# Four-unit attention groups with contexts stored as columns: products of V joined, a wider mask on TensorE, reads of K and Q moved forward

## The chip, the cores and the metric

One core of a Trainium2 chip runs the kernel. The metric is the device time of one execution in microseconds (us). The profiler's names for the engines are PE (TensorE, with PEld for its weight loads), DVE (VectorE), ACT (ScalarE), POOL (GpSimd) and SP (SyncE, which here issues the DMAs).

## The reference

Input x has shape (2, 2048, 512), all in float32. Four blocks follow one another:

```python
# embed: a domain adapter
h = gelu(x @ down.T + b); h = h @ expert[domain].T + ...; x = layernorm(h @ up.T + b + x)
# attention, 16 heads of 32 columns, 2048 queries and keys, 2 batches
y = ln(x) * (1 + scale) + shift
q, k, v = heads(y @ Wq + bq), heads(y @ Wk + bk), heads(y @ Wv + bv)
scores = q @ k.T / sqrt(32) + attention_bias          # bias (2, 16, 2048, 2048)
probs = softmax(where(mask, -inf, scores))
y = y + (probs @ v) @ Wo + bo
# feed-forward 512 -> 2048 -> 512, then a rotation of column pairs and a gated low-rank correction
y = y + gelu2(ln(y) @ W1 + b1) @ W2 + b2
```

The bias alone is 512 MB and is read once.

## The kernel before

The program has three stages, each a block with one instruction list per engine and semaphores between them: `embed_stage`, `attention_stage`, `ffn_stage`. No scheduler is at work. The order on each engine is the order of the calls in the loops at the end of each engine's function.

**Attention** works in units. A unit is 128 queries of one head against all 2048 keys, and there are 512 of them: 2 batches, 2 halves of the queries, 16 heads, 8 units (`RING`). Per unit:

- SP reads the 1 MB tile of the bias into one of eight `tiles` (L1186, L1099) when PE has transposed what was in it.
- POOL adds the negative mask to the first 1920 columns (`pool_columns`, L1249).
- PE computes the scores in two halves (`qk`, L1267), each of two matmuls of 512 columns, into the one score tile `ps_s` in PSUM. To the last 128 columns PE also adds the mask with a matmul of the identity (L1273).
- DVE adds scores and bias and takes the row minimum, one half at a time (`scores`, L1409). PE's next scores of the same half wait for it.
- ACT computes the exponential of the row with its sum (`exp`, L1349).
- PE transposes the probabilities in four chunks of four 128x128 blocks into three PSUM banks in turn (`transposes`, L1288). ACT or DVE copies each chunk to SBUF (`take`, L1359 and L1420). A bank is free for the next chunk but two when it is copied.
- For each pair of units PE multiplies with V (`pv`, L1307). Keys are split in halves, so that two halves of two units fill the four column groups of 32: 32 matmuls, 64 rows in the trace.
- DVE copies the four parts (`parts`, L1444), PE transposes them (`parts_rows`, L1315), and DVE takes reciprocals of the two sums and forms the contexts as rows (`context`, L1428, L1430, L1437). ACT stores them when the sixteen heads are done.

Around a head's eight units SP reads K and Q of the next head (`load_kq`, eight DMAs, L1104 and L1105) behind the first bias tile, and V behind the third.

**FFN** works in eight tiles of 512 tokens. `ctx_columns` (L1787) transposes a tile of contexts, 16 transposes into `ps_t`; ACT copies them (`take_ctx`, L2156); `out_project` (L1975) multiplies with Wo. Then follow the weight products, with weights read in cards of 256 KB, twelve ahead (L1719).

Of the kernel before, what the change touches and what calls it, by code (L numbers as in the profile page):

```python
# [30 lines left out]
P = 128  # L31
# [1016 lines left out]
def attention_buffers(nc, net, ctx, place):  # L1048
# [13 lines left out]
    at.pool_columns = S - 128  # L1062
# [9 lines left out]
    at.p_t = [sb(f"at_prob_t{i}", [P, 2, S // P, P]) for i in range(2)]  # L1072
# [5 lines left out]
    at.cx_sb = sb("at_ctx_parts", [P, P])  # L1078
    at.cx_all = sb("at_ctx_rows", [P, RING, D])
    at.rmin = sb("at_rmin", [P, RING, 2])  # L1080
    at.rsum = sb("at_rsum", [P, RING])
    at.rinv = sb("at_rinv", [P, 2])
# [35 lines left out]
def attention_stage(nc, net):  # L1118
# [9 lines left out]
    NP = NU // 2  # L1128
    KT = S // P
    CH = S // 512  # L1130
    QUART = KT // 2
    TB = 3

# [7 lines left out]
    with ExitStack() as ctx:  # L1141
# [7 lines left out]
        cx_sb, cx_all, rmin, rsum, rinv = net.at.cx_sb, net.at.cx_all, net.at.rmin, net.at.rsum, net.at.rinv  # L1149
# [13 lines left out]
        s_cxs = sem("at_ctx_parts_ready")  # L1163
        s_cxm = sem("at_ctx_summed")
        s_cxo = sem("at_ctx_ready")
        s_rv = sem("at_rinv_ready")
        s_st = [sem(f"at_ctx_stored{i}") for i in range(RING // 2)]
# [9 lines left out]
        def _(sp):  # L1177
# [17 lines left out]
            def load_v(n):  # L1195
                _, _, b, qh, h = place(n * RING)
                after(sp, s_pv, 4 * (n - 1))
                at.read_v(sp, n % 2, b, h)
# [8 lines left out]
            def load_ffn():  # L1207

                for i in range(2):
                    sp.wait_ge(s_st[i], 16)  # L1210
                    sp.wait_ge(s_st[i + 2], 16)
                sp.dma_start(net.cx[:], net.ctx.rearrange("(t j p) d -> t p j d", j=TJ, p=P)[0]).then_inc(net.s_cx, 16)
# [10 lines left out]

            for u in range(at.early, RING):
# [15 lines left out]
            load_ffn()  # L1240

# [11 lines left out]
        def _(pe):  # L1253
# [37 lines left out]
            def pv(pr):  # L1291
                if not 0 <= pr < NP:
                    return

                n = pr * 2 // RING
                after(pe, s_cxo, 2 * pr)
                if pr % 4 == 0:
                    pe.wait_ge(s_vin[n % 2], 16 * (n // 2 + 1))
                for u in (2 * pr, 2 * pr + 1):
# [3 lines left out]
                for i in range(QUART):  # L1303
                    for g in range(4):
                        half, j = divmod(g, 2)
                        t = half * QUART + i
                        last = pe.matmul(ps_c[g * HD:(g + 1) * HD, 0:P], v_sb[n % 2][:, t, :], p_t[pr % 2][:, j, t, :],  # L1307
                                         start=(i == 0), stop=(i == QUART - 1))
                last.then_inc(s_pv, 1)

            def parts_rows(pr):
                if not 0 <= pr < NP:
                    return
                pe.wait_ge(s_cxs, pr + 1)
                pe.transpose(ps_c[:, P:2 * P], cx_sb[:], ident).then_inc(s_cxm, 1)  # L1315

            for g in range(-1, NU // 4 + 1):
                u, pr = 4 * g, 2 * g
                transposes(u, (0, 1))
                qk(u + 3, 1)  # L1320
                parts_rows(pr - 2)
                transposes(u, (2, 3))
                qk(u + 4, 0)
                transposes(u + 1, (0, 1, 2))
                pv(pr - 1)
                qk(u + 4, 1)
                qk(u + 5, 0)
                transposes(u + 1, (3,))
                transposes(u + 2, (0, 1))
                qk(u + 5, 1)  # L1330
                parts_rows(pr - 1)
                transposes(u + 2, (2, 3))
                qk(u + 6, 0)
                transposes(u + 3, (0, 1, 2))
                pv(pr)
                qk(u + 6, 1)
                qk(u + 7, 0)
                transposes(u + 3, (3,))

        @block.scalar  # L1340
        def _(act):
            cxv = net.ctx.rearrange("(b q t p) c -> (b q) p t c", p=P, t=RING, q=QH)

# [8 lines left out]
            def take(u, c):  # L1352
# [3 lines left out]
                pr, j = divmod(u, 2)  # L1356
                after(act, s_pv, pr - 1)
                act.wait_ge(s_pt[k], i + 1)
                act.activation(p_t[pr % 2][:, j, 4 * c:4 * c + 4, :].rearrange("p t q -> p (t q)"), ps_p[k][:],  # L1359
                               ACT.Copy).then_inc(s_pe[k], 1)  # L1360

            def store(pr):
                if not 0 <= pr < NP:
                    return
                if (pr // 4) % HEADS == HEADS - 1:
                    act.wait_ge(s_cxo, 2 * pr + 2)
                    of = slice(2 * (pr % 4), 2 * (pr % 4) + 2)
                    act.dma_start(cxv[pr // (4 * HEADS)][:, of, :], cx_all[:, of, :]).then_inc(s_st[pr % 4], 16)

            for g in range(0, NU // 4 + 1):  # L1370
                u, pr = 4 * g, 2 * g
                take(u - 2, 2)
                take(u - 2, 3)
                exp(u)
                take(u - 1, 1)
                exp(u + 1)
                take(u - 1, 3)
                take(u, 0)
                take(u, 1)
                take(u, 2)  # L1380
# [1255 lines left out]
```

## Time and profile before

| what | value |
|---|---|
| median of 3 runs (lowest, highest) | 3473.58 us (3472.29, 3478.68) |
| the profiled execution, and its span | 3475.8 us, 3474.0 us |
| mean granted clock of TensorE | 0.992 |
| busy: PE, PEld | 3408.8 us (98%), 2692.7 us (78%) |
| busy: DVE, ACT, POOL | 2343.6 us (67%), 2278.9 us (66%), 2395.8 us (69%) |
| embed, attention, FFN, by the first matmul of each stage | to 490.3, to 2495.6, to the end |
| read from HBM, written | 849.63 MB, 99.62 MB |

Attention is 58% of the span, FFN 28%. An engine's busy time is what its instructions took; PE's rows overlap, so the distance from one start to the next tells more than a duration. A line "A <- B" in a list of waits gives how long A stood idle until B released it.

### The profile page before, as it was taken

The numbers are of one execution on the slowest core, as the hardware profiler recorded it, in microseconds if no ns is written. First come the engines' busy times: TensorE is split into PE (matmuls) and PEld (weight loads), VectorE is DVE, ScalarE is ACT, GpSimd is POOL, SyncE is SP. The second block draws the span as 40 slices with busy tenths as digits, with TensorE's granted clock in tenths as the row PEclk, the third lists the DMA queues.
The fourth block names the chain that finished last, engine by engine and source line by source line (L and its number), as shares of the span: only waits on it lengthen the run. The fifth ranks groups of instructions, "written<-read, shape, count | busy, mean of one in ns | idle before, by whom it ended". The sixth has DMA issues, their size and how long they took to land. (4 is left out here: it accounts for less than half of the span.)

```text
span 3474.0 us, 84659 instructions
## 1 busy us (share of the span) xinstructions
PE 3408.8 (98%) x33299; PEld 2692.7 (78%) x33299; DVE 2343.6 (67%) x5039; ACT 2278.9 (66%) x3399; POOL 2395.8 (69%) x942
## 2 busy tenths in 40 slices
PE   7999989999999999999999999999999999999998
PEld 3444448888888888888888888888778888887886
DVE  7776758888888888888888888888623232332333
ACT  2433449999999999999999999999622212221321
POOL 1222249999999999999999999999643324232322
PEclk8999999999999999999999999999999999999998
DMA  6666599888898988898888998888644544564463
GB/s 215 225 235 239 197 367 349 325 337 331 333 401 329 338 331 333 341 389 337 332 332 329 367 370 334 331 327 329 246 144 154 167 137 157 164 191 143 154 210 124
DMA packets 342721, 954.80 MB, mean 275 GB/s; under 512 B 33204, under 2 KB 190004, under 8 KB 267576
## 3 DMA queue, kind: packets, MB, share of 16 engines
q1 hardware_dynamic: 337108, 940.95, 73.4%
q10 hardware_dynamic: 5220, 8.42, 0.6%
q8 instruction: 269, 4.41, 0.5%
q14 instruction: 124, 1.02, 0.1%
HBM read 849.63 MB, written 99.62 MB: 273 GB/s over the span
## 5 line engine op out<-in xcount | busy, mean ns | idle before, releaser
L1249 POOL TENSOR_TENSOR at_tiles<-at_tiles,at_negmask 128x1920 f32<-128x1920 f32 x509 | 1950.7, 3896 | 29.9 <-DMA at_tiles<-in_bias 19.0
L1349 ACT ACTIVATE at_tiles<-at_tiles,at_rmin 128x2048 f32<-128x2048 f32 x512 | 1030.5, 2013 | 2.4 <-DVE at_rmin L1409 2.4
L1288 PE MATMUL at_ps_p<-consts,at_tiles 128*128 128x128 f32 x8192 | 1023.6, 272 | 1.7 <-ACT at_prob_t L1359 1.3
L1288 PEld LDWEIGHTS at_ps_p<-consts,at_tiles 128*128 128x128 f32 x8192 | 936.3, 139 | 72.5 <-DVE at_prob_t L1420 2.0
L1359 ACT ACTIVATE at_prob_t<-at_ps_p 128x512 f32<-128x512 f32 x1664 | 898.2, 603 | 125.0 <-PE at_ps_p L1288 124.9
L1409 DVE CUSTOM_DVE_ANT_0 at_tiles<-at_ps_s,at_tiles,at_rmin 128x1024 f32<-128x1024 f32 x512 | 655.0, 1279 | 171.7 <-PE at_ps_s L1273 171.0
L1267 PE MATMUL at_ps_s<-at_k_stack,at_q_stack 128*128 128x512 f32 x2048 | 700.7, 438 | 8.1 <-DVE at_rmin L1409 6.1
L1409 DVE CUSTOM_DVE_ANT_0 at_tiles<-at_ps_s,at_tiles 128x1024 f32<-128x1024 f32 x512 | 623.9, 1219 | 24.5 <-POOL at_tiles L1249 22.2
L1307 PE MATMUL at_ps_c<-at_prob_t,at_v 128*32 128x128 f32 x16384 | 500.3, 274 | 1.0 <-DVE at_ctx_rows L1437 1.0
L1307 PEld LDWEIGHTS at_ps_c<-at_prob_t,at_v 128*32 128x32 f32 x16384 | 431.6, 110 | 44.2 <-issue 43.0
L1267 PEld LDWEIGHTS at_ps_s<-at_k_stack,at_q_stack 128*128 128x128 f32 x2048 | 310.8, 191 | 62.5 <-issue 51.5
L1420 DVE COPY at_prob_t<-at_ps_p 128x512 f32<-128x512 f32 x384 | 251.9, 683 | 3.0 <-PE at_ps_p L1288 3.0
L1863 PE MATMUL ff_ps_m<-ff_norm_t,ff_w_card 128*128 128x256 f32 x1024 | 234.7, 379 | 1.4 <-ACT ff_feats L2147 0.9
L1863 PEld LDWEIGHTS ff_ps_m<-ff_norm_t,ff_w_card 128*128 128x128 f32 x1024 | 194.2, 190 | 31.1 <-issue 3.3
L2276 POOL TENSOR_TENSOR ff_x<-ff_res,ff_b 128x512 f32<-128x512 f32 x32 | 46.4, 1473 | 229.0 <-DVE ff_x L2447 229.0
L2160 ACT ACTIVATE ff_norm_t<-ff_ps_t,ff_beta_columns,ff_g_columns 128x512 f32<-128x512 f32 (+1 forms) x36 | 23.3, 728 | 255.5 <-PE ff_ps_t L1787 240.2
L633 ACT ACTIVATE em_qk<-em_ps_q,em_bqk 128x512 f32<-128x512 f32 x64 | 44.0, 687 | 190.5 <-PE em_ps_q L446 172.0
L1273 PEld LDWEIGHTS at_ps_s<-at_negmask,ident_bf 128*128 128x128 bf16 x512 | 48.9, 96 | 137.8 <-issue 137.8
L693 POOL TENSOR_TENSOR em_gs_norms<-em_gs_norms,em_half 128x2 f32<-128x2 f32 x32 | 27.9, 871 | 167.1 <-DVE em_gs_norms L747 167.1
L2252 POOL TENSOR_TENSOR ff_hid_sum<-ff_hid_c,ff_hid_d 128x512 f32<-128x512 f32 x32 | 40.6, 1268 | 146.2 <-ACT ff_hid_c L2110 146.2
L2095 ACT ACTIVATE ff_part_m<-ff_ps_m 128x512 f32<-128x512 f32 x32 | 19.1, 597 | 172.9 <-PE ff_ps_m L1863 172.9
L2390 DVE TENSOR_TENSOR ff_hid_c<-ff_ps_m,ff_part_u 128x512 f32<-128x512 f32 x32 | 22.1, 691 | 162.9 <-PE ff_ps_m L1863 162.9
(239 smaller groups left out, 4098.3 us busy)
## 6 DMA issues: line engine op xcount, KB each, us to landing
at_tiles<-in_bias SPq DMA_DIRECT2D x512, 1024.0 KB, 6.3
ff_w_card<-w_mix SPq DMA_DIRECT2D x256, 256.0 KB, 2.7
ff_w_card<-in_W SPq DMA_DIRECT2D x192, 256.0 KB, 2.9
at_k_stack<-k_hi SPq DMA_DIRECT2D x128, 256.0 KB, 5.6
at_k_stack<-k_lo SPq DMA_DIRECT2D x128, 256.0 KB, 5.6
negm<-em_mask_out SPq DMA_DIRECT2D x32, 512.0 KB, 6.5
at_q_stack<-q_hi SPq DMA_DIRECT2D x128, 128.0 KB, 5.3
at_q_stack<-q_lo SPq DMA_DIRECT2D x128, 128.0 KB, 5.3
```

The source lines that it names most:

```text
L633: act.activation(qk32[:, i % 2, :], ps_q[g % 3][:], ACT.Identity, bias=bqk[:, k, c:c + 1]).then_inc(s_qk32, 1)
L1249: pool.tensor_tensor(tiles[s][:, 0:PCOLS], tiles[s][:, 0:PCOLS], negm[s][:, 0:PCOLS], ALU.add).then_inc(s_pool, 1)
L1267: last = pe.matmul(out, q_st[n % 2][:, s * P:(s + 1) * P], k_st[n % 2][:, c * 512:(c + 1) * 512], start=True, stop=not masked)
L1273: last = pe.matmul(ps_s[:, lo:(c + 1) * 512], net.ident_bf[:], negm[s][:, lo:(c + 1) * 512], start=False, stop=True)
L1288: last = pe.transpose(ps_p[k][:, y * P:(y + 1) * P], tiles[s][:, t * P:(t + 1) * P], ident)
L1307: last = pe.matmul(ps_c[g * HD:(g + 1) * HD, 0:P], v_sb[n % 2][:, t, :], p_t[pr % 2][:, j, t, :], start=(i == 0), stop=(i == QUART - 1))
L1349: act.activation(tiles[s][:, :], tiles[s][:, :], ACT.Exp, bias=rmin[:, s, 1:2], scale=-1.0, accum_out=rsum[:, s:s + 1]).then_inc(s_exp, 1)
L1359: act.activation(p_t[pr % 2][:, j, 4 * c:4 * c + 4, :].rearrange("p t q -> p (t q)"), ps_p[k][:], ACT.Copy).then_inc(s_pe[k], 1)
L1409: v.tensor_tensor_reduce(out=half, in0=ps_s[:, a * HALF:(a + 1) * HALF], in1=half, scale=-1.0, scalar=-MAX_FLOOR if a == 0 else rmin[:, s, ...
L1420: v.tensor_copy(p_t[pr % 2][:, j, 4 * c:4 * c + 4, :].rearrange("p t q -> p (t q)"), ps_p[k][:]).then_inc(s_pe[k], 1)
L1863: last = pe.matmul(bank[:, h * HALF:(h + 1) * HALF], left[:, k, h * P:(h + 1) * P], right[:, k, :], start=(m in (1, 2, 5) and h == 0 and k ...
L2276: pool.tensor_tensor(x2[:, j, :], res[:, j, :], b2, ALU.add).then_inc(s_x2, 1)
```

## The change

- Contexts are formed for four units at once. Each of the 16 key blocks of V is multiplied with the probabilities of four units, one per column group, 64 matmuls in one run (128 rows in the trace). The result is the contexts as columns: head dimension and unit on the partitions, queries along the row. No sum of parts is left.
- The probabilities now stand in five single buffers, not two double ones.
- The four row sums get their reciprocals on DVE (`invert`), a copy spreads each over 32 columns, PE transposes the tile (`rinv_columns`), DVE copies it from PSUM (`take_rinv`), and one DVE product of 128 columns gives the contexts (`context`). SP stores them, 64 KB a group, in blocks by head.
- POOL's part of the mask ends at column 1856; PE adds it for 192 columns.
- K and Q of the head after next are read behind the sixth bias tile of each head, and those of the second head ahead of the loop.
- PE's, ACT's and DVE's calls stand in another order; the scores lead the transposes by four units.
- FFN reads a context tile with 16 DMAs in the form that `out_project` needs. The transposes, ACT's copies and their semaphores go. The two banks that `out_project` writes first are swapped in some tiles (`row_bank`).

```diff
-    at.pool_columns = S - 128
+    at.pool_columns = S - 192
-    at.p_t = [sb(f"at_prob_t{i}", [P, 2, S // P, P]) for i in range(2)]
+    at.p_t = [sb(f"at_prob_t{i}", [P, S // P, P]) for i in range(4)]
+    at.p_t += [sb("at_prob_t4", [P, S // P, P])]
+            load_kq(1)
             for n in range(NH):
...
-                        if s == 0:
-                            load_kq(n + 1)
+                        if s == 5 and n + 2 < NH:
+                            load_kq(n + 2)
                         if s == 2:
                             load_v(n + 1)
+                        if s % 4 == 2:
+                            store(2 * n + s // 4 - 1)
...
+            def store(g):
+                n, s, b, qh, h = place(4 * g)
+                sp.wait_ge(s_cxo, g + 1)
+                sp.dma_start(net.ctx[(b * QH + qh) * 2 + s // 4, h], cx_t[g % 2][:]).then_inc(s_st[g % 2], 16)
...
+            def pv(g):
+                pe.wait_ge(s_rc, g + 1)
...
+                for t in range(KT):
+                    for j in range(4):
+                        last = pe.matmul(ps_c[j * HD:(j + 1) * HD, 0:P], v_sb[n % 2][:, t, :], p_t[(4 * g + j) % NPT][:, t, :],
+                                         start=(t == 0), stop=(t == KT - 1))
...
+            def rinv_columns(g):
+                pe.wait_ge(s_rv, 2 * g + 2)
+                after(pe, s_cxo, g)
+                pe.transpose(ps_c[:, P:2 * P], rinv[:].rearrange("p j d -> p (j d)"), ident).then_inc(s_rt, 1)
...
+            def invert(g):
+                s = 4 * g % RING
+                dve.wait_ge(s_exp, 4 * g + 4)
+                after(dve, s_rt, g)
+                v.reciprocal(rinv4[:], rsum[:, s:s + 4]).then_inc(s_rv, 1)
+                dve.wait_ge(s_rv, 2 * g + 1)
+                v.tensor_copy(rinv[:], rinv4[:].unsqueeze(2).broadcast_to([P, 4, HD])).then_inc(s_rv, 1)
+            def take_rinv(g):
+                dve.wait_ge(s_rt, g + 1)
+                v.tensor_copy(rinv_t[:], ps_c[:, P:2 * P]).then_inc(s_rc, 1)
+            def context(g):
+                dve.wait_ge(s_pv, g + 1)
+                dve.wait_ge(s_rc, g + 1)
+                after(dve, s_st[g % 2], 16 * (g // 2))
+                v.tensor_tensor(cx_t[g % 2][:], ps_c[:, 0:P], rinv_t[:], ALU.mult).then_inc(s_cxo, 1)
...
+        def read_ctx(sp, n):
+            blocks = net.ctx[n].rearrange("(c i) (u d) q -> i d c u q", i=P // HD, d=HD)
+            for i in range(P // HD):
+                to = net.cx[i * HD:(i + 1) * HD].rearrange("p c (u q) -> p c u q", q=P)
+                for c in range(DC):
+                    sp.dma_start(to[:, c], blocks[i][:, c]).then_inc(net.s_cx, 16)
...
-            ctx_columns(0)
             out_project(0)
```

PE in the middle of attention, before: one pair of units (the product with V, scores and masks, transposes; `at_ctx_parts` is the tile of the four parts).

```order
L1307 MATMUL at_ps_c<-at_prob_t,at_v 32x128 x32
L1267 MATMUL at_ps_s<-at_k_stack,at_q_stack 128x512 x2
L1273 MATMUL at_ps_s<-at_negmask,ident_bf 128x128
L1267 MATMUL at_ps_s<-at_k_stack,at_q_stack 128x512 x2
L1288 MATMUL at_ps_p<-consts,at_tiles 128x128 x12
L1267 MATMUL at_ps_s<-at_k_stack,at_q_stack 128x512 x2
L1273 MATMUL at_ps_s<-at_negmask,ident_bf 128x128
L1315 MATMUL at_ps_c<-consts,at_ctx_parts 128x128
L1288 MATMUL at_ps_p<-consts,at_tiles 128x128 x8
L1267 MATMUL at_ps_s<-at_k_stack,at_q_stack 128x512 x2
L1288 MATMUL at_ps_p<-consts,at_tiles 128x128 x12
```

PE at the same place after the change, the first half of a group of four. The rest of the group is: four scores in a run with one mask, four transposes, the transposition of the reciprocals (L1329), eight transposes, two scores, eight transposes, two scores with their mask, and four transposes up to the next product.

```order
L1320 MATMUL at_ps_c<-at_prob_t,at_v 32x128 x64
L1303 MATMUL at_ps_p<-consts,at_tiles 128x128 x4
L1282 MATMUL at_ps_s<-at_k_stack,at_q_stack 128x512 x2
L1303 MATMUL at_ps_p<-consts,at_tiles 128x128 x8
L1282 MATMUL at_ps_s<-at_k_stack,at_q_stack 128x512 x2
L1288 MATMUL at_ps_s<-at_negmask,ident_bf 128x192
L1303 MATMUL at_ps_p<-consts,at_tiles 128x128 x8
L1282 MATMUL at_ps_s<-at_k_stack,at_q_stack 128x512 x2
L1303 MATMUL at_ps_p<-consts,at_tiles 128x128 x8
L1282 MATMUL at_ps_s<-at_k_stack,at_q_stack 128x512 x2
L1288 MATMUL at_ps_s<-at_negmask,ident_bf 128x192
L1303 MATMUL at_ps_p<-consts,at_tiles 128x128 x12
```

One product per four units stands where there were two, and one pair of score halves has no mask between them.

DVE after the change, in the same group: the reciprocals and the spreading copy stand between the two score halves of one unit (`ISA` is the scores' instruction; numbers are of buffers).

```order
L1408 ISA at_tiles6,at_rmin<-at_ps_s,at_tiles6 128x1024
L1408 ISA at_rmin 128x1
L1427 RECIPROCAL at_rinv4<-at_rsum 128x4
L1429 COPY at_rinv<-at_rinv4 128x128
L1408 ISA at_tiles6,at_rmin<-at_ps_s,at_tiles6,at_rmin 128x1024
L1408 ISA at_rmin 128x1
L1418 COPY at_prob_t2<-at_ps_p2 128x512
```

Before, DVE had here a reciprocal, a product and two fused products on the parts in PSUM.

## Rows read from the trace of the kernel before

**Rows 1.** Windows, attention: us, busy (instructions) by engine, PEclk, DMA share, GB/s
```profile
560.00:2470.00 1910.00, 1909.92 (x26338) 1619.47 (x26340) 1639.75 (x3570) 1796.71 (x2585) 1890.59 (x494) 1.00 0.89 341
```
**Rows 2.** Waits of PEld, 520 to 2470 us: us in total, times, longest
```profile
PEld at_ps_s L1267 <- DVE at_rmin L1409: 2.2, 10, 0.3
...
PEld at_ps_s L1267 <- DMA at_k_stack<-k_lo: 0.5, 1, 0.5
```
**Rows 3.** Waits of DVE, ACT and POOL, 560 to 2470 us
```profile
DVE at_tiles L1409 <- PE at_ps_s L1273: 168.6, 243, 1.3
...
ACT at_prob_t L1359 <- PE at_ps_p L1288: 113.2, 369, 0.7
...
POOL at_tiles L1249 <- DMA at_tiles<-in_bias: 18.1, 21, 3.7
```
**Rows 4.** Timeline of PE, one pair of units: start us, us from first start to last end
```profile
2448.58 0.73 PE L1267 MATMUL at_ps_s<-at_k_stack,at_q_stack 128*128 128x512 f32 x2
...
2449.74 1.48 PE L1288 MATMUL at_ps_p<-consts,at_tiles 128*128 128x128 f32 x12
2450.97 0.70 PE L1267 MATMUL at_ps_s<-at_k_stack,at_q_stack 128*128 128x512 f32 x2
2451.51 0.23 PE L1273 MATMUL at_ps_s<-at_negmask,ident_bf 128*128 128x128 bf16 x1
2451.58 0.28 PE L1315 MATMUL at_ps_c<-consts,at_ctx_parts 128*128 128x128 f32 x1
2451.70 1.04 PE L1288 MATMUL at_ps_p<-consts,at_tiles 128*128 128x128 f32 x8
2452.49 0.71 PE L1267 MATMUL at_ps_s<-at_k_stack,at_q_stack 128*128 128x512 f32 x2
2453.04 1.48 PE L1288 MATMUL at_ps_p<-consts,at_tiles 128*128 128x128 f32 x12
2454.45 1.95 PE L1307 MATMUL at_ps_c<-at_prob_t,at_v 128*32 128x128 f32 x64
2456.33 0.50 PE L1267 MATMUL at_ps_s<-at_k_stack,at_q_stack 128*128 128x512 f32 x1
```
**Rows 5.** POOL's mask addition, 1200 to 1300 us: ns min/median/max, first and last start
```profile
L1249 POOL TENSOR_TENSOR at_tiles<-at_tiles,at_negmask x27: 3850/3858/3868, 1199.0 to 1298.5; 128x1920 f32<-128x1920 f32 x27
```
**Rows 6.** Timeline of PE in FFN: the transposes of one context tile
```profile
2775.33 1.97 PE L1787 MATMUL ff_ps_t<-consts,ff_ctx 128*128 128x128 f32 x16
2777.13 1.45 PE L1975 MATMUL ff_ps_m<-ff_wo,ff_cols 128*128 128x512 f32 x3
```
**Rows 7.** Timeline of PE, the first scores of the stage
```profile
490.26 1.17 PE L1267 MATMUL at_ps_s<-at_k_stack,at_q_stack 128*128 128x512 f32 x4 [1.68 <-PEq L136]
491.27 0.23 PE L1273 MATMUL at_ps_s<-at_negmask,ident_bf 128*128 128x128 bf16 x1
```
**Rows 8.** SP's issue of the K reads: ns min/median/max, first and last start
```profile
L1104 SPq DMA_DIRECT2D at_k_stack<-k_hi x128: 453/584/699, 452.0 to 2431.1; - x128
```
**Rows 9.** DMA issues: queue, times, KB each, median us to landing
```profile
at_tiles<-in_bias SPq DMA_DIRECT2D x512, 1024.0 KB, 6.3
```
**Rows 10.** Windows, one of three stretches with mask loads (the others alike)
```profile
974.00:1070.00 96.00, 96.00 (x1326) 81.31 (x1318) 81.86 (x179) 90.53 (x131) 90.92 (x25) 1.00 0.98 390
```
**Rows 11.** Timelines: POOL, then DVE beside it in FFN; DVE in embed
```profile
2516.41 1.27 POOL L2276 TENSOR_TENSOR ff_x<-ff_res,ff_b 128x512 f32<-128x512 f32 x1
...
2515.25 0.52 DVE L2353 TENSOR_SCALAR ff_norm<-ff_res,ff_mv,ff_rstd 128x512 f32<-128x512 f32 x1
2516.48 1.48 DVE L2353 TENSOR_SCALAR ff_norm<-ff_res,ff_mv,ff_rstd 128x512 f32<-128x512 f32 x1 [0.71 <-POOL ff_rstd L2293]
...
473.73 0.27 DVE L921 COPY rot_s<-em_sins 128x128 f32<-128x128 f32 x1
473.87 0.27 DVE L922 TENSOR_SCALAR rot_s<-em_sins 128x128 f32<-128x128 f32 x1
```

More of the change, by code:

```diff
@@ L1309, in pv @@
                 last.then_inc(s_pv, 1)
-            def parts_rows(pr):
-                if not 0 <= pr < NP:
+            def rinv_columns(g):
+                if not 0 <= g < NG:
                     return
[L1314 to L1327, printed above, removed]
+                pe.wait_ge(s_rv, 2 * g + 2)
+                after(pe, s_cxo, g)
+                pe.transpose(ps_c[:, P:2 * P], rinv[:].rearrange("p j d -> p (j d)"), ident).then_inc(s_rt, 1)
@@ L1433, in context @@
-                after(dve, s_st[s // 2], 16 * (n // HEADS))
-                dve.wait_ge(s_rv, 2 * pr + 2)
-                for j in range(2):
-                    own = slice(j * HD, (j + 1) * HD)
-                    v.scalar_tensor_tensor(cx_all[:, s + j, h * HD:(h + 1) * HD], ps_c[:, P + 2 * HD:2 * P][:, own],
-                                           rinv[:, j:j + 1], cx_sb[:, own], ALU.mult, ALU.add).then_inc(s_cxo, 1)
-            def parts(pr):
-                if not 0 <= pr < NP:
-                    return
-                dve.wait_ge(s_pv, pr + 1)
-                v.tensor_copy(cx_sb[:], ps_c[:, 0:P]).then_inc(s_cxs, 1)
@@ L1446, in _ @@
-            for g in range(-1, NU // 4 + 1):
-                u, pr = 4 * g, 2 * g
-                context(pr - 2)
-                scores(u + 3, 1)
-                scores(u + 4, 0)
-                take(u + 1, 0)
-                parts(pr - 1)
-                scores(u + 4, 1)
-                scores(u + 5, 0)
-                context(pr - 1)
-                scores(u + 5, 1)
-                scores(u + 6, 0)
-                take(u + 3, 2)
-                take(u + 3, 0)
-                scores(u + 6, 1)
-                parts(pr)
-                scores(u + 7, 0)
+                s = 4 * g % RING
@@ new lines, in context @@
+            def context(g):
+                if not 0 <= g < NG:
+                    return
+                dve.wait_ge(s_pv, g + 1)
+                dve.wait_ge(s_rc, g + 1)
+                after(dve, s_st[g % 2], 16 * (g // 2))
+                v.tensor_tensor(cx_t[g % 2][:], ps_c[:, 0:P], rinv_t[:], ALU.mult).then_inc(s_cxo, 1)
+            for g in range(-5, NG + 1):
+                u = 4 * g
+                scores(u + 17, 0)
+                scores(u + 17, 1)
+                scores(u + 18, 0)
+                invert(g + 3)
+                scores(u + 18, 1)
+                take(u + 14, 3)
+                scores(u + 19, 0)
+                scores(u + 19, 1)
+                take(u + 16, 0)
+                take_rinv(g + 3)
+                scores(u + 20, 0)
+                scores(u + 20, 1)
+                context(g + 3)
+                take(u + 17, 0)
```

211 lines of the change are left out of this document (87 added, 124 removed).

## The prediction

> **What bounds the kernel now.** I began with the page's busy shares in the table above: PE 98%, POOL 69% over the whole span, ACT and DVE less. The windows view says more: from 560 to 2470 us, the attention stage, PE is busy in every microsecond, POOL for 1890.59 of 1910, ACT for 1796.71 and DVE for 1639.75 [rows 1]. Four engines are near their limits, so the waits decide who leads. PE waits 2.2 us for DVE's scores and 0.5 us for a K load [rows 2], while DVE waits 168.6 us for PE's scores and ACT 113.2 us for PE's transposes [rows 3]. PE sets the pace; POOL follows closely, with 18.1 us of waiting for bias loads.
>
> PE's order repeats every two units. From the first score row at 2448.58 to the same one at 2456.33 is 7.75 us [rows 4], so 15.50 us for four units, 128 such groups. POOL's pace is shorter: 27 instructions start between 1199.0 and 1298.5, 3.827 us apart, 15.31 for four [rows 5]. It is 1.2% faster than PE and no more.
>
> In FFN PE is again the bound, and the transposes of the context are a stretch of its row: 2775.33 to 2777.13 [rows 6].
>
> **The change on PE, from start-to-start distances of [rows 4].** A new group of four consists of:
> - three pairs of score matmuls with a mask between transposes: 2450.97 to 2451.58 is 0.61, three are 1.83. The mask is 192 columns for 128; a pair of 512-column matmuls needs 0.55, so 64 columns are about 0.03, times four masks 0.12.
> - three pairs without a mask: 2452.49 to 2453.04, 0.55 each, 1.65.
> - one run of four score matmuls with its mask: 490.26 to 491.27 is 1.01 up to the mask [rows 7], and 0.07 for the mask, 1.08.
> - transposes: five runs of eight at 0.79 (2451.70 to 2452.49), 3.95; a run of twelve at 1.23; three runs of four at a third of that, 1.23; one of them stands ahead of the context product, where twelve took 1.41 and not 1.23, so 0.18 more.
> - one transposition of the reciprocals, 0.12, where two of the parts stood.
> - the context product of 128 rows. Today 64 rows take 1.88 with both edges (2454.45 to 2456.33); their starts lie (1.95 - 0.27) / 63 = 0.027 apart, so 64 more add 1.71: 3.59.
>
> The sum is 14.98 against 15.50. The arithmetic is the same; what goes is one of two entries and exits of the context product. A transpose run behind a product is not in these rows and may cost a tenth more than I gave it: I take 15.0, a gain of **0.5 us a group, 64 us** (bounds 50 and 68).
>
> **POOL.** 1856 columns for 1920 make 3.827 x 0.967 = 3.70 us a unit, 14.80 a group. Its lead over PE stays at about 1.2%; without this edit POOL at 15.31 would be the bound.
>
> **ACT and DVE.** ACT's exponentials and copies are as many as before: 1796.71 / 1910 x 15.5 = 14.58 us a group, in 15.0. DVE loses ten small instructions a group and gets four. Neither is the bound, but both stand within tenths of PE where four transposed banks wait during the long product. I give 0.06 us a group, 8 us (bounds 0 and 30).
>
> **FFN.** Sixteen transposes per tile go, 1.80 us each time [rows 6], eight tiles: **14.4 us** (12 to 16; the first tile runs after idle time). ACT's four copies of each tile were beside other work. SP now issues 16 reads for one: a K read in attention holds it 0.58 us [rows 8], so 9 to 10 us, behind which card loads queue; twelve cards are loaded ahead, each worth 1.7 us of PE, which covers it. Without that cover it would be 10 us a tile.
>
> **K and Q earlier, context stores.** PE waited 0.5 us for K in the stage [rows 2]: nothing to win. The stores are 64 KB each on SP, where a wait for the context holds back the next bias load; the context of that group is finished three units before. Nothing, and up to 5 us lost.
>
> **Bias loads.** PE reads ahead: the scores of unit u+4 now follow the transposes of unit u a good two microseconds earlier than before. That is the time in which a bias tile must land (6.3 us [rows 9]) and POOL must add the mask (3.7): 10.1 of about 13 us. In the three stretches in which masks are loaded, DMA is busy 98% at 390 GB/s, and POOL loses 5 us of 96 while PE loses nothing [rows 10]. With less in hand PE will lose some 2 us in each: 6 us (bounds 0 and 15). The Trainium skill ("DMA: Bandwidth & Descriptors", Where 436 GB/s comes from) has about 358 GB/s as the limit of a core on HBM. By that rule these stretches could not run at 390 even now; the trace disagrees, so the sum has no such term. By the rule alone it would be some 30 us worse.
>
> **The copy that spreads the reciprocals.** This is the part that speaks against the change. It is DVE's first instruction in the stage that is a plain copy from SBUF to SBUF. Rows show what such an instruction meets: at 2516.48 a DVE TENSOR_SCALAR between SBUF tiles starts 0.07 us after a POOL addition of 1.27 us and takes 1.48 instead of 0.52, that is, it waits until POOL has finished [rows 11]. And copies of 128 columns from one repeated element start 0.14 us apart, about half of what one column per cycle would take if 512 columns need 0.6, so this form probably runs in the fast mode too [rows 11]. In attention POOL runs one 3.7 us addition behind the other. The Trainium skill ("SBUF — State Buffer", SBUF: two separate sides) calls this pair of ports an exclusive lock, held for the whole instruction; the trace agrees, by that one row.
>
> The copy stands between the two score halves of a unit, and the next score matmul of PE waits for the second half: by the rows above DVE has about 0.2 us to spare there. If the copy met POOL at random, it would wait half of 3.7, 1.85, and PE 1.65 of it. But four POOL additions (14.80, and some 0.15 for the copy's hold) are as long as PE's group (15.0). After one stall PE and DVE stand later by just what the copy waited, and the next copy comes near POOL's boundary again. The two can fall into step. Then only slips and late loads are passed on: I take 0.14 us a group, **18 us lost** (bounds 0 and 1.65 x 128 = 211).
>
> **Sum.** -64 + 8 - 14.4 + 6 + 18 = -46 us. The profiled execution took 3475.8 (span 3474.0); its 3430 is 2 above what the median of the runs, 3473.6, would give. I forecast **3430 us**; its own range is 3412 to 3455.
>
> **Rivals.**
> 1. *The copy is not held by POOL* (it does not run in the two-port mode, or slips through). Against: [rows 11]. For: only one such row, and none in attention. Then 18 us less lost, and less to 3410.
> 2. *The copy is held and finds no step* (slower). Place: DVE's copy after the first half of every fourth unit's scores. Price: 1.65 us a group where it meets POOL at random, and about 1.2 where POOL waits for loads now and then and so is idle in some of the meetings. 15.0 becomes 16.2 to 16.65 against today's 15.50, +90 to +147 us; the gain of FFN (14.4) and the small losses on ACT and in the mask stretches (8 and 6) cancel. That makes 3564 to 3620. It decides from a mean wait of the copy of about 0.7 us: there the 0.5 us of gain is gone. For it: a late landing or an early POOL addition moves the boundary, and when POOL gets ahead of the copy's start by a hair, the copy waits 3.7 us at once.
> 3. *The long product starves ACT.* It has 0.42 us of idle time left in a group. If it waits 0.9, the gain in attention is gone and FFN's remains: 3461.
> 4. *Bias tiles come late.* If landing rises from 6.3 to over 9 us, POOL misses its turn in every group: 3490 and more. DMA's share of 0.89 in the stage [rows 1] would go to 0.92; the negmask stretches show that even 0.98 costs POOL 5 us in 96.
>
> **Chances.** In step 0.42; rival 1 0.16; rival 2 0.34; rival 3 0.04; rival 4 0.04. A run of this kernel tells 0.2% (7 us) from no change. In step, a twentieth ends within it. So faster 0.60, same 0.04, slower 0.36. The range goes down to the case without any stall and with every gain at its bound, 3398, and up into the middle of rival 2, 3575, where with the rest of rival 2 some 0.17 is left out.
>
> **What the profile would show.** PE's period of four units 15.0 to 15.3; two runs of 64 product rows joined; POOL's additions 3.70 apart. The row of the spreading copy: near 0.3 us in rival 1, a few tenths more in step, 1.5 to 2 us in rival 2, with PE then waiting for DVE's scores over 100 us in all. FFN shorter by 14 us whatever attention does. If the copy's row is short and PE still waits, my account of the lock is wrong; if PE's period is over 15.3 with no wait, my sum from the distances is.

## The result and the profile after

The changed kernel takes **3756.86 us** (median of 4 runs, 3751.28 to 3774.65) against 3474.62 (4 runs): ratio **1.082**, 95% interval 1.079 to 1.084, 282 us slower. The prediction was 3430, its range 3398 to 3575. The profiled execution took 3751.28, span 3749.5.

| | before | after |
|---|---|---|
| first score matmul to last context matmul, us | 1999.9 | 2291.7 |
| from there to the end, us | 983.9 | 965.1 |
| mean granted clock of TensorE | 0.992 | 0.970 |
| PE idle in gaps over 0.25 us between these two, added up from its records | 9 | 240 |

All of the loss is in attention; what follows it gained 19 us. Parts 1 and 5 of the changed kernel's page; in part 5 a group's busy time and mean stand ahead of the bar, the idle time before it and what ended most of that behind it:

```profile
PE 3450.4 (92%) x33043; PEld 2726.8 (73%) x33043; DVE 2467.4 (66%) x4271; ACT 2285.1 (61%) x3367; POOL 2335.7 (62%) x942
...
L1264 POOL TENSOR_TENSOR at_tiles<-at_tiles,at_negmask 128x1856 f32<-128x1856 f32 x509 | 1891.2, 3746 | 379.8 <-DMA at_tiles<-in_bias 367.6
...
L1429 DVE COPY at_rinv<-at_rinv 128x128 f32<-128x128 f32 x128 | 261.5, 2043 | 4.4
```

The waits in attention (560 to 2740 us: total, times, longest), to hold against [rows 2] and [rows 3]:

```profile
ACT at_prob_t L1371 <- PE at_ps_p L1303: 371.2, 455, 5.4
POOL at_tiles L1264 <- DMA at_tiles<-in_bias: 360.8, 169, 6.1
...
PE at_ps_s L1282 <- DVE at_rmin L1408: 213.0, 116, 3.2
```

Three readings. The spreading copy, L1429, takes 2.04 us in the mean for work of 0.23 us, its shortest row. PE now waits 213 us for DVE's scores, 116 times in some 122 groups. And POOL, the engine that holds the copy, waits 361 us itself, for bias tiles, where it was 18.1 [rows 3]: my sum had 6 us for late bias tiles, and those in the mask stretches alone.

One group shows the chain. The timeline of DVE and then POOL (start, duration, engine, line):

```profile
1181.94 0.17 DVE L1427 RECIPROCAL at_rinv<-at_rsum 128x4 f32<-128x4 f32 x1
1182.15 3.58 DVE L1429 COPY at_rinv<-at_rinv 128x128 f32<-128x128 f32 x1
1185.65 1.27 DVE L1408 CUSTOM_DVE_ANT_0 at_tiles<-at_ps_s,at_tiles,at_rmin 128x1024 f32<-128x1024 f32 x1
...
1181.92 7.40 POOL L1264 TENSOR_TENSOR at_tiles<-at_tiles,at_negmask 128x1856 f32<-128x1856 f32 x2
```

POOL begins an addition at 1181.92, the copy comes 0.23 us later and is done at 1185.73, 0.09 us after that addition. In the changed kernel 118 of the 128 copies are held, and each of them ends 0.08 to 0.10 us after an addition's end. The second score half follows, 3.4 us late, and PE stands still. The windows of the same stretch (engines' busy time, then PEclk, DMA share, GB/s):

```profile
1184.00:1186.50 2.50, 0.00 (x0) 0.00 (x0) 2.50 (x2) 1.22 (x4) 2.50 (x2) 1.00 0.97 382
...
1189.00:1191.00 2.00, 2.00 (x10) 1.70 (x9) 1.98 (x5) 1.85 (x2) 0.32 (x1) 0.50 0.97 406
1192.00:1193.00 1.00, 1.00 (x9) 0.70 (x7) 0.22 (x3) 0.69 (x2) 0.62 (x1) 1.00 1.01 413
```

Here PE stands idle for 3.1 us, to 1187.0, and 1.4 us after it is at work again the granted clock falls from full (2.4 GHz) to half (1.2 GHz) for 3.4 us. Attention has 42 such stretches in the changed kernel; of the 24 times that PE idles for over 3 us, 11 are followed by one, so not every long stall pays it. Over attention, 560 to 2740 us, the windows give a mean clock of 0.96 where it was 1.00 [rows 1]: 0.04 x 2180 = 87 us, give or take 10 for the rounding, that the halved stretches cost. That is a price of a stall that I had left out.

### The profile page after: what moved, and what is told of

The parts are those of the page before. It is cut to its first block and busy times, and to the rows that moved or that the text cites. A ratio compares the mean times of both kernels' runs of the same rounds, so it can differ in the third digit from the quotient of the medians.

```text
span 3749.5 us, 83709 instructions
## 1 busy us (share of the span) xinstructions
PE 3450.4 (92%) x33043; PEld 2726.8 (73%) x33043; DVE 2467.4 (66%) x4271; ACT 2285.1 (61%) x3367; POOL 2335.7 (62%) x942
## 5 line engine op out<-in xcount | busy, mean ns | idle before, releaser
L1264 POOL TENSOR_TENSOR at_tiles<-at_tiles,at_negmask 128x1856 f32<-128x1856 f32 x509 | 1891.2, 3746 | 379.8 <-DMA at_tiles<-in_bias 367.6
L1371 ACT ACTIVATE at_prob_t<-at_ps_p 128x512 f32<-128x512 f32 x1664 | 919.8, 598 | 393.2 <-PE at_ps_p L1303 390.5
L1303 PE MATMUL at_ps_p<-consts,at_tiles 128*128 128x128 f32 x8192 | 1146.0, 282 | 3.4 <-ACT at_prob_t L1371 1.8
L1303 PEld LDWEIGHTS at_ps_p<-consts,at_tiles 128*128 128x128 f32 x8192 | 976.5, 146 | 90.7 <-issue 35.5
L1282 PE MATMUL at_ps_s<-at_k_stack,at_q_stack 128*128 128x512 f32 x2048 | 752.9, 450 | 228.9 <-DVE at_rmin L1408 223.2
L1320 PE MATMUL at_ps_c<-at_prob_t,at_v 128*32 128x128 f32 x16384 | 476.7, 273 | 12.8 <-issue 10.0
L1418 DVE COPY at_prob_t<-at_ps_p 128x512 f32<-128x512 f32 x384 | 263.9, 687 | 73.9 <-PE at_ps_p L1303 73.5
L1429 DVE COPY at_rinv<-at_rinv 128x128 f32<-128x128 f32 x128 | 261.5, 2043 | 4.4
L1443 DVE TENSOR_TENSOR at_ctx_t<-at_ps_c,at_rinv_t 128x128 f32<-128x128 f32 x128 | 37.4, 292 | 307.4 <-PE at_ps_c L1320 307.4
L1288 PE MATMUL at_ps_s<-at_negmask,ident_bf 128*128 128x192 bf16 x512 | 134.8, 263 | 0.0
```

Of the source, the lines that this page charges most:

```text
L1264: pool.tensor_tensor(tiles[s][:, 0:PCOLS], tiles[s][:, 0:PCOLS], negm[s][:, 0:PCOLS], ALU.add).then_inc(s_pool, 1)
L1282: last = pe.matmul(out, q_st[n % 2][:, s * P:(s + 1) * P], k_st[n % 2][:, c * 512:(c + 1) * 512], start=True, stop=not masked)
L1288: last = pe.matmul(ps_s[:, lo:(c + 1) * 512], net.ident_bf[:], negm[s][:, lo:(c + 1) * 512], start=False, stop=True)
L1303: last = pe.transpose(ps_p[k][:, y * P:(y + 1) * P], tiles[s][:, t * P:(t + 1) * P], ident)
L1320: last = pe.matmul(ps_c[j * HD:(j + 1) * HD, 0:P], v_sb[n % 2][:, t, :], p_t[(4 * g + j) % NPT][:, t, :], start=(t == 0), stop=(t == KT - 1))
L1371: act.activation(p_t[u % NPT][:, 4 * c:4 * c + 4, :].rearrange("p t q -> p (t q)"), ps_p[k][:], ACT.Copy).then_inc(s_pe[k], 1)
```

## The experiments

Three theories were open: **A**, the copy is held by POOL and costs PE the wait and the clock; **B**, the new order takes bias tiles too late; **C**, the new order starves ACT. All kernels are compared with the kernel before on the same chip, at 3474 to 3476 us. The edits are shown shortened.

**One RECIPROCAL in place of reciprocal and copy (e1).**
```diff
-v.reciprocal(rinv4[:], rsum[:, s:s + 4]).then_inc(s_rv, 1)
-dve.wait_ge(s_rv, 2 * g + 1)
-v.tensor_copy(rinv[:], rinv4[:].unsqueeze(2).broadcast_to([P, 4, HD])).then_inc(s_rv, 1)
+v.reciprocal(rinv[:], rsum[:, s:s + 4].unsqueeze(2).broadcast_to([P, 4, HD])).then_inc(s_rv, 2)
```


> The changed kernel, but one RECIPROCAL reads the four sums spread over 128 columns and writes the 128 reciprocals; the plain copy is gone, everything else stays. Theory A, the lock: the copy waits for POOL's addition (its row has a mean of 2.04 us, 1.8 more than the 0.23 of its shortest), PE idles 1.87 us a group for it and then runs for a while at the low clock. A RECIPROCAL in before took 0.16 us beside 246 additions, so it should take about 0.3 us here, PE's group should fall from 17.8 to 15.0 to 15.3 us and the time to 3400 to 3450 us. Theory B, late bias tiles: POOL waits 380 us for bias loads in the changed kernel and 30 in before; if the longer read-ahead of the scores is the cause and the copy only stands where it shows, the time stays over 3650. Theory C, the order of PE's transposes leaves ACT without work (322 us of waiting): over 3600.

Measured: 3552.72 us, ratio 1.023 (1.021 to 1.024). The copy and its waiting are 204 us of the loss, but not all. The RECIPROCAL of 128 columns takes 0.95 us each of its 128 times (0.941 to 0.951), always alike and so never held, three times what I expected from the 0.16 of four columns. POOL still waits 172 us for bias tiles over the kernel. B is alive for the rest.

**A copy added to the kernel before (e2).**
```diff
                 scores(u + 5, 0)
+                v.tensor_copy(spare[:].rearrange("p (j d) -> p j d", j=3),
+                              consts[:, C_IDENT:C_IDENT + 3].unsqueeze(2).broadcast_to([P, 3, HD]))
                 context(pr - 1)
```


> The kernel before with one more instruction on DVE in every group of four units: a copy of three elements, each spread over 32 of 96 columns, from SBUF to SBUF, between the two score halves of a unit; nobody reads its result. Theory A, the lock alone costs it: the copy waits for POOL's addition of 3.9 us as in the changed kernel, about 1.9 us each time; DVE waits 1.3 us a group for PE today, which takes some of it, so PE loses 0.5 to 1.9 us a group and up to 0.9 more at the low clock: 3540 to 3800 us. It would be near 3480 only if the copies fell into step with POOL. Theories B and C (the order, the loads): the order is that of before, so 3474 to 3485.

Measured: 3475.25 us, ratio 1.0001 (0.9991 to 1.001). The count of the copy's rows, its duration (min/median/max) and form:

```profile
L1450 DVE COPY at_spare<-consts x128: 243/248/249, 511.8 to 2479.7; 128x96 f32<-128x96 f32 x128
```

None of 128 was held, though 127 start while an addition of POOL runs, and at every phase of it. The theory as I had it, a plain copy between SBUF tiles is held, is wrong.

**Four columns only (e3), added to e1.**
```diff
+v.tensor_copy(rinv4[:], rsum[:, s:s + 4]).then_inc(s_rv, 1)
```


> e1_one_reciprocal with a plain copy of four columns (sums to an unused tile, SBUF to SBUF) behind the reciprocal, where the spreading copy stood. Theory A: the wait does not depend on the copy's size, so its row has a mean near 1.9 us and the time is that of the changed kernel, 3700 to 3790 us. Rival: a copy so small is not held, or is held only for its share; then its row is near 0.1 us and the time is that of e1.

Measured: 3754.74 us (one run), as the changed kernel. The same view:

```profile
L1428 DVE COPY at_rinv<-at_rsum x128: 104/1410/6214, 516.1 to 2781.5; 128x4 f32<-128x4 f32 x128
```

A copy of four columns, 0.10 us by itself, is held much as one of 128 is (mean 1.49 for 2.04), and the time is the same. Size does not free it. What differs between this one and the free copy is four elements for three.

**POOL's addition in two halves (e4).**
```diff
-pool.tensor_tensor(tiles[s][:, 0:PCOLS], tiles[s][:, 0:PCOLS], negm[s][:, 0:PCOLS], ALU.add)
+pool.tensor_tensor(tiles[s][:, 0:PCOLS // 2], ...)
+pool.tensor_tensor(tiles[s][:, PCOLS // 2:PCOLS], ...)
```


> The changed kernel, with POOL's addition of 1856 columns issued as two of 928. Theory A: the copy waits only until the half that is running has ended, at most 1.9 us and 0.9 in the mean; PE's idle time falls from 1.87 to about 0.7 us a group and the clock falls less often: 3500 to 3620 us. Theories B and C: nothing on the path is shorter, POOL has one more start-up a unit: 3757 or more.

Measured: 3653.9 us (one run), 103 less than the change but 34 above my bound. The copy's median falls to 0.61 us, its mean only to 1.34, because 10 are held for longer than one half of 1.97 us, the longest 13.6 us. More on that below.

**Five elements in place of four (e5).** This asks whether the form decides.
```diff
-at.rinv4 = sb("at_rinv4", [P, 4])
-at.rinv = sb("at_rinv", [P, 4, HD])
+at.rinv4 = sb("at_rinv4", [P, 5])
+at.rinv = sb("at_rinv", [P, 5, HD])
...
-v.tensor_copy(rinv[:], rinv4[:].unsqueeze(2).broadcast_to([P, 4, HD])).then_inc(s_rv, 1)
+v.tensor_copy(rinv[:], rinv4[:].unsqueeze(2).broadcast_to([P, 5, HD])).then_inc(s_rv, 1)
```


> The changed kernel with the spreading copy reading five elements (four reciprocals and a constant) and writing 160 columns in place of four and 128; the transposition takes the first 128. The copy of three elements into 96 columns that ran beside POOL without any wait took 0.248 us, about what one column per cycle needs; the copies of four elements waited for POOL in both kernels that have them. Theory: only the form that reads two columns at once takes the lock, and an odd number of elements does not get it. Then the copy takes 0.31 us, never more, and PE's group loses 0.6 us against the 16.20 of e1_one_reciprocal: 15.5 to 15.7, 3465 to 3510 us, with POOL still waiting for the bias tiles of slots 6 and 7. Rival: not the form but the kernel's phase kept the copy of 96 columns free; then it waits about 2 us again and the time is 3740 to 3770.

Measured: 3550.14 us, ratio 1.021 (1.019 to 1.023). The copy:

```profile
L1430 DVE COPY at_rinv<-at_rinv x128: 319/320/323, 518.6 to 2579.6; 128x160 f32<-128x160 f32 x128
```

It is never held: the form decides. DVE's part between the two score halves is also some 0.4 us shorter than in e1 (RECIPROCAL of four and copy, 0.17 and 0.32, for 0.95), for a gain of 2.6 us, within the spread: what remains is not on DVE. I had put it there. In this kernel the bias tile of slot 6 is issued 2.8 us (median) after its buffer comes free and POOL starts it 0.07 us after it lands; other slots but 7 are issued after 0.09.

**The form alone, in the kernel before (e11).** The edit against e2:
```diff
-v.tensor_copy(spare..., j=3), consts[:, C_IDENT:C_IDENT + 3].unsqueeze(2).broadcast_to([P, 3, HD]))
+v.tensor_copy(spare..., j=4), consts[:, C_IDENT:C_IDENT + 4].unsqueeze(2).broadcast_to([P, 4, 24]))
```


> e2_copy_in_before with four elements spread over 24 columns each where it has three over 32: 96 columns to 96 columns in both, same place, same tiles. Theory A with the form: the even number takes the fast mode and with it the lock, so its row rises from 0.25 us to about 2 us in the mean, and the kernel before becomes slower; DVE has 1.3 us a group of waiting in hand, so 0.5 to 1.5 us a group, 3540 to 3700 us. Rival: the order of before (or the constant it reads) kept the copy free, not the form: 0.25 us and 3472 to 3478. A third way: it is held, but what it waits is taken up by DVE's waiting: a long row and 3475 to 3500.

Measured: 3630.55 us (median of 3 runs, 3579.95 to 3631.71; a fourth took 3675.0), ratio 1.040 (1.034 to 1.046), and the copy:

```profile
L1450 DVE COPY at_spare<-consts x128: 200/1923/16072, 512.2 to 2636.4; 128x96 f32<-128x96 f32 x128
```

The same 96 columns at the same place: 3 x 32 in 0.25 us always, 4 x 24 in 0.20 at best and 1.92 in the median, 123 of 128 held. That is the lock by itself, shown. "VectorE: DVE Perf Modes" of the Trainium skill (Mode 2×_2P) gives the condition: one source and the destination in SBUF, and their outermost dimensions that are not one both even, or odd and equal. The traces agree in every case here. Their records have the destination as one run of columns, so the counts to compare are 4 and 128, 4 and 96, 4 and 4, which are held, and 3 and 96, 5 and 160, which are not. I had cited the lock and not this condition, which would have told me how to leave it out.

**K and Q back to their place (e6).** The change reads them two heads ahead in the sixth unit of a head. SP's own timeline there (engine SPq is its queue):

```profile
1251.53 0.46 SPq L1106 DMA_DIRECT2D at_k_stack<-k_hi  x1
...
1255.85 0.59 SPq L1107 DMA_DIRECT2D at_q_stack<-q_lo  x1
1256.56 0.52 SPq L1101 DMA_DIRECT2D at_tiles<-in_bias  x1
```

Eight reads hold SP from 1251.5 to 1256.4, and the bias tile of the next slot goes out behind them.
```diff
-            load_kq(1)
...
-                        if s == 5 and n + 2 < NH:
-                            load_kq(n + 2)
+                        if s == 0:
+                            load_kq(n + 1)
```


> The changed kernel with K and Q read as before, one head ahead in the first unit of a head and not two ahead in its sixth. The copy stays. Theory D, the place of the eight K and Q reads: they hold SP for 4.6 us, in the changed kernel just where the bias tile of slot 6 could be issued (2.8 us late, its landing 7.1 us after issue where 5.4 before), and POOL starts that tile 0.07 us after it lands every time; so POOL's lateness falls and the time with it by 30 to 100 us, to 3650 to 3730, the held copy (2 us mean) still costing most. If POOL is no longer set back once a head it may fall into step with the copy, and the time would be 3480 to 3560. Rival: the place of the reads costs nothing, as the prediction had it: 3750 to 3760.

Measured: 3669.69 us, ratio 1.056 (1.054 to 1.058): 87 us of the loss. The copy is still held (median 1.75 us, up to 3.8), and PE's group is 17.2 us in the mean against 15.5 in e7 below. It found no step.

**Both edits (e7)**: the diffs of e5 and e6 together.

> Both edits together: the copy of five elements and K and Q read as before. If the lock and the place of the reads are all that went wrong, PE's group is what its undisturbed groups in the changed kernel show, 15.2 to 15.5 us, and the time 3430 to 3475 us, at or below the kernel before. If something else is wrong too (ACT without work, PE's order), it stays over 3490 with PE waiting for another engine in every group.

Measured: **3457.69 us**, ratio **0.9952** (0.9937 to 0.9967): the fastest kernel here, 0.5% faster than the kernel before. Its waits (560 to 2450 us) and the copy:

```profile
POOL at_tiles L1264 <- DMA at_tiles<-in_bias: 79.0, 61, 4.0
...
PE at_ps_p L1303 <- issue: 10.6, 8, 2.5
PE at_ps_c L1320 <- issue: 8.8, 12, 2.0
...
PE at_ps_s L1282 <- DVE at_rmin L1408: 2.4, 4, 0.9
```

The four kernels form a square, and its two effects add up almost exactly:

| us | K, Q in the sixth unit | K, Q in the first |
|---|---|---|
| copy of four | 3756.9 (the change) | 3669.7 |
| copy of five | 3550.1 | 3457.7 |

The held copy costs 207 and 212 us, the place of the reads 87 and 92. C falls: ACT's wait for PE goes from 371 to 107 us with no edit of its order. Of B little is left: POOL still waits 79.0 us for bias tiles where it was 18.1 [rows 3], but PE waits only 2.4 us for the scores behind them.

**The reads moved in the kernel before (e8).**
```diff
+            load_kq(1)
...
-                        if s == 0:
-                            load_kq(n + 1)
+                        if s == 5 and n + 2 < NH:
+                            load_kq(n + 2)
```


> The kernel before with K and Q read two heads ahead in the sixth unit, as the change does, and nothing else. In before the tile of slot 6 lies ready 4.3 us in the median before POOL takes it (a tenth of the time 7.4 or more). Theory D: it is issued 2.8 us later and lands 2 us slower, so POOL waits now and then, and with PE's lead over POOL of 0.2 us a group part of that reaches PE: 3480 to 3540 us. Rival (the prediction's nothing): 3472 to 3478.

Measured: 3478.88 us, ratio 1.0015 (1.0005 to 1.0025), 5 us and not 90. My nothing was nearly right for the old order. In the kernel before, a tile of slot 6 lies ready for some 4.5 us (median) before POOL takes it; here it is issued 3.1 us late and still lies ready for 0.4. POOL waits 25.7 us in place of 18.1 and PE 3.3. In the new order with the reads in their old place (e7) that margin is 2.1 us, less than the 2.8 by which the moved reads delay the issue. So the reads' place costs only together with the new order. That it is the earlier scores which use the margin up is argued, no run has them alone.

**The reads spread over four units (e10)**, in the kernel of e5.
```diff
-                        if s == 5 and n + 2 < NH:
-                            load_kq(n + 2)
+                        if s >= 4 and n + 2 < NH:
+                            load_kq_part(n + 2, s - 4)
```


> The changed kernel with the copy of five elements, and with K and Q read two heads ahead as the change has it, but two of the eight reads in each of the units 4, 5, 6 and 7 of a head. Theory D1: what cost 92 us between e5 and e7 is that eight reads in a row hold SP for 4.6 us, longer than POOL's 3.75 us a unit, ahead of the bias tile of slot 6. Spread out they hold it 1.2 us at a time: 3440 to 3470 us, as e7 or a little less. Rival D2: it is when the 1.5 MB move (in the second half of a head, where POOL's next tiles come with the least in hand), not the hold: then the time is 3500 to 3550, near e5.

Measured: 3469.89 us (3465.11 to 3477.72), ratio 0.9986 (0.9977 to 0.9995). 80 of the 92 us come back with the reads still two heads ahead in the second half: it was the block on SP. All slots are issued 0.1 us after they come free. In e7 the block of reads (5.4 us) hides behind slot 0: PE's long product follows, and the next tile comes free only 6.6 us later, where slot 6 follows slot 5 after 2.8. The last 12 us are not settled.

**The product in two halves (e9)**, in the kernel of e7.
```diff
+                pv(g, 0)
                 qk(u + 8, 1)
                 transposes(u + 4, (3,))
-                pv(g)
+                pv(g, 1)
```


> e7_five_and_kq with the context product of a group in two halves of eight key tiles each, one pair of score matmuls and four transposes between them. In e7 PE idles 29 us in all in gaps over 0.25 us in which the profile shows nothing awaited, 23 of 27 of them inside or just behind the long product, each 0.5 to 2 us behind the start of a 16 KB packet of the instruction queue; before has 4 us of such gaps. Theory F: the product's 256 instructions in 3.4 us outrun the loading of PE's code; cut in two with other work between, the gaps should shrink to under 8 us, against 128 more edges of the product at 0.17 us (22 us): 3430 to 3465 us, near e7 in total. Rival: the gaps have another cause (a bank of PSUM, a wait that is not shown); they stay near 29 us and the time rises by the edges to 3475 to 3490.

Measured: 3528.24 us, ratio 1.016 (1.014 to 1.017), far outside both. The first half pushes DVE's scores back: DVE waits 207 us for PE's scores, and PE 30.5 us for the reciprocals. The gaps for which nothing is shown fall by half, from 20.1 us in e7 (22 waits) to 10.6 (18), but so much else has moved that this is weak evidence. It fits theory F and doesn't settle it.

**POOL's columns put back to 1920 (e12)**, in the kernel of e7.
```diff
-    at.pool_columns = S - 192
+    at.pool_columns = S - 128
```


> e7_five_and_kq with POOL's share of the mask put back to 1920 columns, PE's to 128. The prediction said that without this edit POOL would be the bound at 15.31 us a group. By the rows of before and of e7 an addition takes 3.90 against 3.75 us, so POOL has 15.6 us of work in a group of four where PE's undisturbed group is 15.2, and at 1920 columns each late bias tile adds to it: 128 groups at 15.7 to 15.9 against 15.5 in e7 make 3480 to 3510 us. Rival: PE gets back 0.03 us for each mask product (0.12 a group, 15 us) and POOL's lead is still enough: 3440 to 3455 us.

Measured: 3465.38 us, ratio 0.997 (0.996 to 0.998), between my two cases; 8 us above e7, or 6 by the two ratios, for the two were taken on different chips. The median group is 15.25 us, as in e7. For the expectation I had taken POOL's duration (3.90) for its pace; the pace of 1920 columns is 3.83 [rows 5], four in 15.31, and PE's mean group (15.5) leaves POOL time to catch up. The prediction's "POOL would be the bound" was too strong: the edit is worth some 6 to 8 us.

## Why the prediction was wrong

**The copy: right mechanism, wrong case.** The prediction's main step, "the two can fall into step", failed. In the place of 0.14 us a group stand 1.65: the square gives 207 to 212 us, and my upper bound was 1.65 x 128 = 211. Rival 2, at 0.34, is what happened. That its 1.65 meets the measured total is in part luck. With the copy freed, PE's waits for the scores fall from 213.0 to 50.7 us (the change to e5) and from 170.5 to 2.4 (e6 to e7), by 162 and 168 us: 1.3 to 1.4 a group over some 122 groups, between rival 2's two prices of 1.2 and 1.65. The rest is the clock, which I hadn't priced: its mean in attention rises from 0.976 to 0.996 between e6 and e7, worth 44 us. Rival 2's total of 3564 to 3620 was too low even for e6, which has the held copy without the moved reads and takes 3670, for that clock and for PE's own terms below. The argument for the step was that four additions are about as long as PE's group. They are near (3.71 apart, so 14.83, against 15.2), but where POOL runs without a wait the copy after a held one comes 0.2 to 0.3 us *behind* a boundary, the worst place, where a wait is a whole addition: so it was at 1182.15. And POOL does not run free: it waits for bias tiles 169 times, and each wait moves the boundary. The waits came out spread from 0 to 3.4 with a mean of 1.8, half of an addition, as chance would have it. Why no step was found is argued from this, no run shows it by itself.

My idea of a step was not empty, though. In e11, in the old order, where DVE has 1.3 us a group in hand, one could be seen up to 1040 us: copies of 0.95 and of 1.8 to 2.5 us in turn, most groups at 15.5 to 16.4. One long miss at 1041 ended it, and for 900 us most copies took over 3 us and most groups 17.6 to 19.1. From 1950 us on the step was back (39 of 42 groups under 16.5 us). The copy's rows, from the miss on and from 1949.2 on:

```profile
L1450 DVE COPY at_spare<-consts x52: 204/3379/16072, 1041.4 to 1949.2; 128x96 f32<-128x96 f32 x52
L1450 DVE COPY at_spare<-consts x44: 200/915/3965, 1949.2 to 2636.4; 128x96 f32<-128x96 f32 x44
```

So even there the step came and went, and what decides between the two states is open. In step e11 still loses about 0.5 us a group (16.02 against 15.51 from 1950 us on), not the 0.14 that I took.

One reading ahead of this was wrong too. From 512 columns in 0.6 us, 128 need 0.15, so copies 0.14 us apart [rows 11] were no sign of the fast mode. The sign is in the runs: 128 columns in 0.23 us at best, but 96 in 0.25 where the source count is 3.

Part of the price was the clock, which the prediction did not name. PE's idle gaps in attention are 240 us in the change and 32 in e7, a difference of 208; the halved clock takes 90 and 8 us there by its records, 82 more: together 290, against 291 between the two stages' lengths (2291.7 and 2000.9).

**K and Q earlier: "nothing to win", a sign overlooked.** I had the rule in the text, that SP's issues count where they stand, and priced it at nothing because PE does not wait for K. The cost is on the queue, not on the engine that reads the tile: 4.9 us of SP where POOL turns every 3.71 and where the tile's margin is 2.1 (e7). Rival 4 (bias tiles late) had the right place, at 0.04 and with the wrong cause; I looked for it in DMA's bandwidth. It measured 87 to 92 us with the new order and 5 with the old.

**PE's group: 15.0 taken, 15.15 to 15.26 measured** in the undisturbed groups of e7. The product is 3.63 (3.59 was taken), runs of eight transposes 0.79 as taken; the run of four score matmuls takes 1.24 with its mask where I took 1.08 from [rows 7], since the second half waits 0.3 us for DVE each time. With 15.2 the gain is 0.3 x 128 = 38 us, not 64. And 35 of e7's groups take over 15.35, 37 us more in sum than at 15.2: the gain is gone, and attention takes 2000.9 us in e7 against 1999.9. Part of those 37 are the gaps told of at the end.

**FFN: 14.4 taken**, 18.6 to 18.8 measured from the last context matmul to the end (983.9 to 965.1 and 965.2). Of the 4 us that I missed, 2.6 lie at the border of the stages: from the last context matmul to the first matmul of FFN it is 5.5 us before and 2.8 after. The 16 reads on SP cost nothing that shows.

**ACT, the stores, the mask stretches.** No run gives ACT a price; e7's waits show PE under 1 us for it.

So e7, which has neither fault, gains +1.0 - 18.6 = -17.6 us, all of it behind attention. Rival 1's 3410 was the forecast for such a kernel; it is 3458.

The signs announced held: the copy's row at 2.04 us was next to rival 2's (1.5 to 2), and PE's waits for the scores stood at 213 us, over the 100 named.

## What to carry to other kernels

Before a one-source DVE instruction is put beside a busy POOL, look at its form: a copy within SBUF whose outermost counts were both even waited until POOL's addition had ended, whatever its size; an odd source count, at 160 columns for 128 and 0.09 us more than its fastest row, set it free and was worth 207 us. A queue's block of issues belongs where the next buffer comes free last, and a margin must be counted once for all edits that use it: the moved reads cost 5 us in the old order and 90 in the new. And don't count on a step between two engines with nearly equal periods where one of them waits for third parties: the changed kernel never found one, and e11 lost it for 900 us. Take the random meeting as the forecast, and add the clock that the stalls cost.

## What the runs showed of the hardware

**A held copy can lose its turn more than once.** In e11, after the mask loads, one copy of 96 columns took 16.07 us. DVE's row, and POOL's additions from 1041 to 1057.8 (durations min/median/max, first and last start):

```profile
1041.36 16.07 DVE L1450 COPY at_spare<-consts 128x96 f32<-128x96 f32 x1
```

```profile
L1250 POOL TENSOR_TENSOR at_tiles<-at_tiles,at_negmask x5: 3824/3825/3882, 1038.4 to 1053.5; 128x1920 f32<-128x1920 f32 x5
```

POOL's additions went on at their pace, and the copy ended with the fifth. In e4, with halves, the longest took 13.6 us and 14 of 111 held copies outlasted more than one half; in e3 the longest took 6.2. In the changed kernel all 118 held copies went in after the first addition's end; what makes one lose is open. "SBUF — State Buffer" (SBUF: two separate sides) of the Trainium skill says that whichever starts first has the ports for the whole instruction; the trace agrees, and shows besides that the one that waits isn't always next.

**PE's code may come late.** The context product is 256 PE instructions in 3.6 us, loads included. Its timeline in two groups of e7, a clean one and the next (the last bracket is idle time and what ended it):

```profile
1034.28 3.70 PE L1320 MATMUL at_ps_c<-at_prob_t,at_v 128*32 128x128 f32 x128
...
1049.53 3.54 PE L1320 MATMUL at_ps_c<-at_prob_t,at_v 128*32 128x128 f32 x121
1054.24 0.42 PE L1320 MATMUL at_ps_c<-at_prob_t,at_v 128*32 128x128 f32 x7 [1.16 <-issue]
```

From 560 to 2490 us e7 has 21 gaps over 0.25 us for which the profile shows nothing awaited, 20 us in all. By the records of the packets 17 of them, 14 us, begin 0.3 to 2.2 us after the start of a packet of 16 KB on the instruction queue (1.1 us here), where such packets start some 9 us apart; many lie four groups from the next. The expectation for e9 named 23 of 27 such gaps and 29 us; by this count it is less. "Runtime: NRT & Kernel Launch" (Instruction fetch mechanics) of the Trainium skill has code fetched in blocks of 16 KiB, which is 256 instructions, and the crossing as mostly hidden. The block size agrees with this trace; if the gaps are such crossings, they are not hidden, at 0.3 to 2.5 us each, beside a DMA that is busy 90% of the time. That late code is the cause is argued from this and from e9's halving, and is not shown.

**A RECIPROCAL isn't a copy in price**: 0.17 us for 4 columns and 0.95 for 128 (e1), 6.3 ns a column between the two, where the copy of 160 columns takes 0.32 (e5).
